# Quarters between an extra unit's two maxima, block 1's rows ahead of values, later padding, a head in halves and shifted zero products in a convolution/attention/MoE kernel on one core

## Time and profile before

| what | us |
|---|---|
| median of 3 runs | 241.24 |
| the runs | 241.24, 239.71, 246.65 |
| the profiled execution, device time | 239.72 |
| span of its trace | 237.9 |
| PE busy | 227.8 (96%) |
| DVE busy | 200.2 (84%) |
| ACT busy | 172.5 (72%) |
| POOL busy | 45.5 (19%) |

### The profile page before, as it was taken

How to read it: one execution, slowest core, us unless ns; L and a number is a source line. 1 busy time by engine, 2 the same in 40 slices (tenths; PEclk the granted TensorE clock), 3 DMA queues, 4 the chain that set the end, 5 groups by cost and what they waited for, 6 DMA issues and landing times.

```text
span 237.9 us, 6170 instructions
## 1 busy us (share of the span) xinstructions
PE 227.8 (96%) x2361; PEld 126.3 (53%) x2361; DVE 200.2 (84%) x425; ACT 172.5 (72%) x347; POOL 45.5 (19%) x80
## 2 busy tenths in 40 slices
PE   8899999999999999999999999999999998789994
PEld 6356455455555555555555555555444785558521
DVE  5899998999999999999999999999722593348874
ACT  3553759898999998899889998999996432228810
POOL 8956069400000000200000300030000000000160
PEclk9999999999999999999999999999999999999999
DMA  5005510161131120451300000000000000000002
GB/s 142 2 8 206 132 19 3 30 236 27 53 92 45 50 68 26 105 154 69 98 9 1 4 3 1 6 0 1 4 3 0 3 0 3 1 3 0 1 0 91
DMA packets 6082, 10.09 MB, mean 42 GB/s; under 512 B 2236, under 2 KB 3820, under 8 KB 5924
## 3 DMA queue, kind: packets, MB, share of 16 engines
q1 hardware_dynamic: 5908, 9.63, 13.7%
q10 hardware_dynamic: 144, 0.07, 0.1%
HBM read 6.84 MB, written 2.62 MB: 40 GB/s over the span
## 4 chain that ended last, share of the span: by engine, by line
PE 87%; POOL 5%; DVE 5%; issue 1%; ACT 1%; DVEq 0%; POOLq 0%; ACTq 0%
PE psum L598 26%; PE psum L494 17%; PE psum L530 17%; PE psum L636 4%; PE psum L916 3%; DVE half_max L1307 2%; POOL kop L958 1%; POOL qop L958 1%; PE psum L563 1%; PE psum L435 1%; PE psum L826 1%; PE psum L556 1%; PE psum L452 1%; POOL early L1039 1%; PE psum L470 1%; PE psum L816 1%
## 5 line engine op out<-in xcount | busy, mean ns | idle before, releaser
L1307 DVE TENSOR_REDUCE half_max<-psum 128x1 f32<-128x512 f32 x256 | 156.0, 678 | 2.1 <-PE psum L494 1.8
L1125 ACT ACTIVATE probs<-psum 128x512 f32<-128x512 f32 x228 | 120.0, 601 | 10.7 <-PE psum L530 6.5
L494 PE MATMUL psum<-kop,qop 64*128 64x512 f32 x256 | 87.4, 442 | 0.7 <-DVE kop L1274 0.6
L530 PE MATMUL psum<-qop,kop 64*128 64x512 f32 x256 | 83.0, 441 | 0.5 <-ACT qop L1130 0.4
L598 PE MATMUL psum<-probs,v_aug 128*32 128x256 f32 (+1 forms) x1312 | 73.1, 339 | 0.2 <-DVE o_sb L1321 0.2
L494 PEld LDWEIGHTS psum<-kop,qop 64*128 64x128 f32 x256 | 40.7, 184 | 19.9 <-DVE half_max L1307 12.6
L530 PEld LDWEIGHTS psum<-qop,kop 64*128 64x128 f32 x256 | 39.4, 184 | 20.5 <-ACT probs L1125 11.4
L598 PEld LDWEIGHTS psum<-probs,v_aug 128*32 128x32 f32 x1312 | 32.7, 109 | 30.2 <-issue 20.1
L1018 POOL CAST max_part<-negmax 128x8 fp32r<-128x8 f32 x13 | 2.5, 189 | 92.0 <-issue 81.3
L1059 POOL TENSOR_TENSOR early<-probs,early 128x512 f32<-128x512 f32 x4 | 5.1, 1275 | 56.7 <-ACT probs L1219 55.2
L1121 ACT ACTIVATE probs<-psum 128x1024 f32<-128x1024 f32 x14 | 13.4, 1027 | 0.5 <-PE psum L530 0.4
(11 more groups left out here) (192 smaller groups left out, 195.6 us busy)
## 6 DMA issues: line engine op xcount, KB each, us to landing
parts_scratch<-early SPq DMA_DIRECT2D x4, 512.0 KB, 3.8
qop<-parts_scratch SPq DMA_DIRECT2D x28, 64.0 KB
vt_sb<-in_vt SPq DMA_DIRECT2D x1, 1024.0 KB, 4.8
kop<-parts_scratch SPq DMA_DIRECT2D x14, 64.0 KB
kop<-parts_scratch SPq DMA_DIRECT2D x28, 32.0 KB
x_sb<-in_x SPq DMA_DIRECT2D x2, 256.0 KB, 3.6
q_pair<-in_q_pairs SPq DMA_DIRECT2D x1, 512.0 KB, 3.6
qop<-max_row SPq DMA_DIRECT2D x26, 4.0 KB
```

What stands on the lines that cost most here:

```text
L494: last = nc.tensor.matmul(psum[:, m % MAX_BANKS, :], qop[at, b * PP + pp, qh * NH + t * P:qh * NH + (t + 1) * P], kop[at, b * PP + pp, c * ...
L530: last = nc.tensor.matmul(psum[:, bank, :], kop[at, b * PP + pp, mt * P:(mt + 1) * P], qop[at, b * PP + pp, qh * NH:(qh + 1) * NH], start= ...
L1125: last = nc.scalar.activation(probs[:, n % P_RING, h, :], psum[:, bank, :], ACT.Exp, scale=SCALE)
L1307: V.tensor_reduce(half_max[:, i, c, h * HT + t:h * HT + t + 1], psum[:, m % MAX_BANKS, :], AX_X, ALU.max, negate=True).then_inc(S["slot_fr ...
```

## The change

- **Head in halves.** The first product takes only columns 0 to 255 of q half 0 (bank 4); columns 256 to 511 come behind k half 0, in bank 2 (`SECOND_BANK`). ACT no longer waits for DVE's `rep_dve`.
- **Quarters between the maxima.** In the extra units of g = 0 and 1 the product of queries and keys stands between the unit's two maxima; at g = 0 four products of zeros (and a wait for `v_out`) stand in front of the first.
- **Block 1's rows in front of the values** at place 8.
- **Later padding.** `pad(1)` stands in the turn of block 2, behind that block's split and three small MEMSETs.
- **Late zero products.** Two in front of the first wide stage's values, whose wait for `st_done` now stands ahead of them; five before the last output's transpose, two before `project(1)`, three for two before `mean_ready`.
- **z by twos.** Of the four transposes two stand in front of the wait for `u_ready`, two behind the layer's last product.

```diff
+CHUNK_BANKS = (4, 5, 6, 7)
+SECOND_BANK = 2
...
+        SECOND_ROWS = phase_end_from(PAIRS_OF * len(CATCH_UP))
...
+            def replicated(i, bank, first, end):
+
+                what, hf = CHUNKS[i]
+                nc.tensor.matmul(psum[:, bank, 0:end - first], w_rep[:, int(what == "k"), :],
+                                 x_sb[:, hf * NH + first:hf * NH + end], start=True, stop=True).then_inc(S["rep_full"], 1)
+
             pe.wait_ge(S["w_rep_ready"], 1)
-            for i, (what, hf) in enumerate(CHUNKS):
-                if what == "k":
-                    pe.wait_ge(S["k_rep_ready"], 2)
-                pe.wait_ge(S[f"in_x{hf}"], 16)
-                nc.tensor.matmul(psum[:, 4 + i, :], w_rep[:, int(what == "k"), :], x_sb[:, hf * NH:(hf + 1) * NH],
-                                 start=True, stop=True).then_inc(S["rep_full"], 1)
-                if i == 0:
-                    rep_constants()
+            pe.wait_ge(S["in_x0"], 16)
+            replicated(0, CHUNK_BANKS[0], 0, QB)
+            rep_constants()
+            pe.wait_ge(S["k_rep_ready"], 2)
+            replicated(1, CHUNK_BANKS[1], 0, NH)
+            replicated(0, SECOND_BANK, QB, NH)
+            pe.wait_ge(S["in_x1"], 16)
+            replicated(2, CHUNK_BANKS[2], 0, NH)
+            replicated(3, CHUNK_BANKS[3], 0, NH)
...
             def after_pair(p):
 
+                if p == SECOND_ROWS:
+                    small_work(p)
                 if p in values_goal:
                     values_until(values_goal[p])
-                small_work(p)
+                if p != SECOND_ROWS:
+                    small_work(p)
...
                     if part_ == 0:
+                        max_half(v, 0)
+                        if g == 0:
+                            pe.wait_ge(S["v_out"], 2)
+                            fill(FILL // 2, PV_BANK, 0, True)
                         pe.wait_ge(S["in_wqk1"], 16)
                         half_queries_and_keys(1, hf, 0, st_free(("qk", hf, 0)))
+                        max_half(v, 1)
                     else:
+                        max_half(v, 0)
                         half_queries_and_keys(1, hf, 1, st_banks(st_index["qk", hf, 0])[0]).then_inc(S["st_full"], 1)
-                    for c in range(HALVES):
-                        max_half(v, c)
+                        max_half(v, 1)
...
             units(first_wide + 2, first_wide + 3)
+            pe.wait_ge(S["st_done"], wide_at)
+            keep_warm(2, WIDE_SMALL)
             values_until(2 * (first_wide - 1))
-            pe.wait_ge(S["st_done"], wide_at)
             rows_of_max(LAST, WIDE_SMALL).then_inc(S["late_rows_full"], 1)
...
             values_until(2 * UNITS)
+            keep_warm(5, PROJ_BANKS[1])
             output_to_tokens(LAST_OUT, ATTN_T_BANKS[1]).then_inc(S["last_full"], 1)
             project(0)
             attn_to_channels(1)
             attn_to_channels(2)
+            keep_warm(2, PV_BANK)
             project(1)
...
-            keep_warm(2, PV_BANK)
+            keep_warm(3, PV_BANK)
             pe.wait_ge(S["mean_ready"], 1)
...
                     by_image(7, w_l, tt_l if l else eye2_sb).then_inc(S["tt_full"], 1)
+                    if l < 2:
+                        tokens_to_channels(4 * l)
                     pe.wait_ge(S["u_ready"], l + 1)
                     by_image(5, w_l, u_l).then_inc(S["gram_full"], 1)
                     if l < 2:
-                        tokens_to_channels(l)
+                        tokens_to_channels(4 * l + 2)
...
                     pool.wait_ge(S["parts1"], hf + 1)
-                    if hf == HALVES - 1:
-                        pad(1)
+                if blk == DIRECT:
+                    pad(1)
...
             act.wait_ge(S["rep_full"], 2)
-            first_part(1, 0, NH)
-            act.wait_ge(S["rep_dve"], 1)
-            first_part(0, QB, NH)
+            first_part(1, CHUNK_BANKS[1], 0, NH)
+            act.wait_ge(S["rep_full"], 3)
+            first_part(0, SECOND_BANK, QB, NH)
```

More of the change, by code:

```diff
@@ L545, in first_rows, with fill @@
                 rows_of_max(blk, st_free(("max_r", blk, 0))).then_inc(S["st_full"], 1)
-            def fill(bank, at, start):
-                for _ in range(FILL):
+            def fill(n, bank, at, start):
+                for _ in range(n):
                     nc.tensor.matmul(psum[:, bank, at:at + P], idle[:, 0:P], idle[:],
@@ L671, in _ @@
                     pe.wait_ge(S["parts0_in"], 2 * HALVES)
-                    fill(ST_BANKS[1], 0, True)
+                    fill(FILL, ST_BANKS[1], 0, True)
             first_rows(0)
@@ L794, in _, with tokens_to_channels @@
             last.then_inc(S["gram0_full"], 1)
-            def tokens_to_channels(c):
-                for t in range(4 * c, 4 * c + 4):
-                    last = nc.tensor.transpose(psum[:, PROJ_BANKS[c], (t % 4) * P:(t % 4 + 1) * P], z[:, t, :], ident)
-                last.then_inc(S["zt_full"], 1)
+            def tokens_to_channels(first):
+                for t in range(first, first + 2):
+                    last = nc.tensor.transpose(psum[:, PROJ_BANKS[t // 4], (t % 4) * P:(t % 4 + 1) * P], z[:, t, :], ident)
+                if t % 4 == 3:
+                    last.then_inc(S["zt_full"], 1)
             def by_image(bank, left, right):
@@ L1072, in _, with first_part @@
                 nc.scalar.activation(rep_rows(w_rep, 1, i), head_weights(1, i), ACT.Copy).then_inc(S["k_rep_ready"], 1)
-            def first_part(i, first, end):
+            def first_part(i, bank, first, end):
                 what, hf = CHUNKS[i]
                 w = int(what == "k")
-                nc.scalar.activation(rep_part[:, i, first:end].bitcast(F32R), psum[:, 4 + i, first:end], ACT.Identity,
+                nc.scalar.activation(rep_part[:, i, first:end].bitcast(F32R), psum[:, bank, 0:end - first], ACT.Identity,
                                      bias=rep_cols[:, 4 + w:5 + w], scale=rep_cols[:, 2 + w:3 + w]).then_inc(S["rep_act"], 1)
@@ L1082, in _ @@
             act.wait_ge(S["rep_full"], 2)
-            first_part(1, 0, NH)
-            act.wait_ge(S["rep_dve"], 1)
-            first_part(0, QB, NH)
+            first_part(1, CHUNK_BANKS[1], 0, NH)
+            act.wait_ge(S["rep_full"], 3)
+            first_part(0, SECOND_BANK, QB, NH)
             for i in (2, 3):
-                act.wait_ge(S["rep_full"], i + 1)
-                first_part(i, 0, NH)
+                act.wait_ge(S["rep_full"], i + 2)
+                first_part(i, CHUNK_BANKS[i], 0, NH)
             act.wait_ge(S["rep_cols_ready"], 3)
-            nc.scalar.activation(rep_q1, psum[:, 4 + BY_POOL_CHUNK, :], ACT.Identity,
+            nc.scalar.activation(rep_q1, psum[:, CHUNK_BANKS[BY_POOL_CHUNK], :], ACT.Identity,
                                  bias=rep_cols[:, 0:1]).then_inc(S["rep_act"], 1)
@@ L1268, in _, with second_part @@
             dve.wait_ge(S["rep_part_ready"], 1)
-            def second_part(i, first, end):
+            def second_part(i, bank, first, end):
                 what, hf = CHUNKS[i]
@@ L1274, in second_part @@
                 V.scalar_tensor_tensor(out=(kop if w else qop)[:, 0, hf * NH + first:hf * NH + end],
-                                       in0=psum[:, 4 + i, first:end], scalar=rep_cols[:, w:w + 1],
+                                       in0=psum[:, bank, 0:end - first], scalar=rep_cols[:, w:w + 1],
                                        in1=rep_part[:, i, first:end], op0=ALU.add, op1=ALU.add).then_inc(S["rep_dve"], 1)
-            second_part(0, 0, QB)
+            second_part(0, CHUNK_BANKS[0], 0, QB)
             dve.wait_ge(S["rep_act"], 1)
-            second_part(1, 0, NH)
+            second_part(1, CHUNK_BANKS[1], 0, NH)
             dve.wait_ge(S["rep_act"], 2)
-            second_part(0, QB, NH)
+            second_part(0, SECOND_BANK, QB, NH)
             dve.wait_ge(S["rep_act"], 3)
-            second_part(2, 0, NH)
+            second_part(2, CHUNK_BANKS[2], 0, NH)
             def denominators(blk):
@@ L1351, in _ @@
             late_copy(LATE + 1)
-            dve.wait_ge(S["rep_full"], len(CHUNKS))
+            dve.wait_ge(S["rep_full"], len(CHUNKS) + 1)
             dve.wait_ge(S["qk_full"], HALVES)
```

4 lines of the change are left out of this document (2 added, 2 removed).

## The result

| | before | after |
|---|---|---|
| median, 20 runs each | 240.43 | 237.86 |
| fastest run | 239.17 | 237.33 |
| profiled execution | 239.72 | 237.35 |
| span of its trace | 237.9 | 235.5 |

The ratio of after to before is 0.9918, with a 95% interval of 0.9894 to 0.9943: 0.8% faster, clear of noise and under the 2% that the forecast called about what can be told from no change. The forecast was 238.5, in a range of 237.0 to 241.8. The four rows of the table don't move alike: 2.57 us by the medians, 1.84 by the fastest runs, 2.37 by the profiled executions and 2.4 by their spans; the part on the prediction says why.

A forecast was written before the change was run, and what follows sets the result against it. The prediction took DVE to bound the maxima stage and ACT the wide stage. Head -0.2, quarters -0.3, rows -0.4, padding -0.25, zero products +0.1 and +0.05, z -0.2 sum to -1.2: 239.72 to 238.5 us, range 237.0 to 241.8.

The forecast's parts named there:

- the 2% class: Whole kernel: a change within about 2% (4.8 us), which a measurement can't tell from no change; chance 0.91.
- the account of the maxima stage: Maxima stage, 10.14 to 169.07 us: DVE bounds it at 0.60 us a reduction, with only about 3.5 us of slack.
- everything reaches its bound: Rival, whole kernel: all gains reach their bounds, 2.5 us together, so 237.2; needs no late second maximum; chance 0.06.
- Room of 1 us to block 3: Later padding: MEMSETs run from about 43 to 50, block 3's maxima are ready about 51.1, leaving 1 us.
- anything won before 43.47 would be lost: Block 2's split, held by POOL's padding until 43.47: earlier gains after block 1's split at 31.72 would be lost again.
- PE's 0.40 goes, and of DVE's 0.69 some 0.3 stay: Block 1's rows: PE's wait at 34.93 vanishes, DVE's delay at 36.71 shrinks; -0.4 us, bounds 0 and -0.69.
- what is late next: Quarters at g = 0: the second maximum comes at 26.4, DVE is ready at 26.03, so some 0.3 us late.
- as long as the fast pace sets in when it does now: Head: condition on the forecast of -0.2 us and its bounds of 0 and -0.5.
- The slow rival: Head: fast pace waits until after about 9 us, costing 3.0 us there, so 241.8 in all; chance 0.10.
- the last rival: Other executions: late zero products stop clock falls in PE's gaps; median gains over 2% at the same 238.5; chance 0.04.
- Absorbed: Rival: a shifted DVE finds PE late elsewhere; only padding and z stay, less 0.15 for zero products: 239.4; chance 0.18.

## Why the prediction was right, and where it was not

The direction, the 2% class and the range held, and so did the account of the maxima stage. The size did not: the profiled execution moved by -2.37 us against -1.2 forecast, the fastest runs by -1.84, the ratio gives 0.8% or about -2.0, and the medians of 20 runs each -2.57. The profiled 237.35 is nearer to the rival *everything reaches its bound* (237.2, a chance of 0.06) than to the forecast, and not by the way the rival names: the quarters stayed short of their bound, the rows and the head went beyond theirs. About 0.5 us of the 2.37 is luck of the one profile (the head, below).

*Right, and shown by undoing:* the maxima stage stands on DVE and everything behind is relative to it, so that each 0.1 us shows at the end (quarters 0.39 in the trace, 0.32 in fastest runs; rows 0.78 and 0.78). POOL's padding held block 2's split, and its move lets the rows pass (0.33 alone, 1.11 with the rows). Room of 1 us to block 3 (1.03). z by twos, 0.2. Zero products at the last transpose hide (forecast +0.1, measured 0); the two in the wide stage, put at 0, cost 0.06.

*What passes through the padding: one step, not three.* The prediction has the 0.9 us of head, quarters and rows pass only because of the later padding, and says that anything won before 43.47 would be lost. But POOL's chain starts at block 1's `negmax` and takes 12.5 us from there (30.94 to 43.47 before, 33.52 to 46.05 with the early padding), so it moves along with whatever is won ahead of that `negmax`. Only the rows, which lie inside it, were held. The sum of the forecast doesn't change by this.

*The rows, -0.4 forecast, -0.78 measured.* The step "PE's 0.40 goes, and of DVE's 0.69 some 0.3 stay" failed. It counted PE's wait of 0.40 and not that the score behind the wait ran alone; in the new order it runs beside a maximum, and the second 0.4 us go too. The measured -0.78 lies outside the bound of -0.69 by 0.1. This is the largest mis-sized term that the kernel owes to the change itself.

*The quarters, -0.3 against -0.39.* The mechanism held, but "what is late next" was too dark: no idle time of 0.3 appears before the second maximum. The four zero products cost 0.20 where the step had 0.3.

*The head, -0.2 against -0.81, outside the bound of -0.5.* The bound was tied to "as long as the fast pace sets in when it does now", and it did not: the rise of the granted clock is stored at 5.65 us in the profile before and at 4.19 in the one after. At 4.19 PE still works at the idle products, which are the same in both kernels, and the first product of the changed head starts only at 4.52; so the change can't have caused this earlier rise, and what it gave is luck of that execution. The nearest pair with like moments is the kernel before (rise at 5.65, first reduction at 10.14) and the halved head with the rows behind (5.52, 9.86): 0.28 us, of which the earlier rise may have a part. So the forecast's 0.2 was near for the split itself, and some 0.5 of the 0.81 come from the clock. This fits the table of the result: 2.37 less 0.5 is close to the 1.84 of the fastest runs. What the old head does behind a rise near 4.2 us no profile shows.

With the halved head the first reduction is at 9.20 to 9.86 in four profiles (rise at 4.1 to 5.5) and at 11.75 to 12.20 in four others (rise at 9.4 to 10.3); with the old head at 10.14 to 10.29 in three (5.65 to 5.87) and at 12.14 in one (10.4). The Trainium skill, "TensorE: Matmul & The Clock Gate", Part 1, has the moment vary by about 0.5 us from run to run. The traces agree that it varies, but not with the size: within the early group it spreads by 1.8 us, and the late group lies 3.5 us and more behind it, which costs about 2.5 us of total time.

*The slow rival was real, but not for the kernel as a whole.* It had 0.10 as the case that decides the median. Its price was 3.0 us from the head; the measured one is 2.7 (12.03 against 9.33), and it meets part of the executions: 6 of the kernel after's 18 runs below 243 lie at 239.7 to 240.3, 12 at 237.3 to 237.9. Whether the halved head makes it more frequent is the more important question. Of the eight kernels with the halved head and 30 idle products 30 of 77 runs lie 2 us or more above their kernel's fastest, against 2 of 16 of the two with the old head and the rest of the change (the kernel with four more products, 0 of 5, is not in this sum). The old head also stands in the kernel before and in the padding alone: 11 of 71 and 1 of 8. On each chip the halved head has more: 14 of 28 against 3 of 32, 6 of 21 against 5 of 23, 4 of 10 against 6 of 40. That points to yes, as the rival argued. It is counted by times, not by profiles, and so not proven. What the split is worth in the median is therefore not shown: 237.97 with the old head (six runs, none late), 237.86 with the new. The median of the 12 early runs is 237.5, so that it looks like 0.5 in those; but their early rises, which are not of the split's making, are in that number. By the 0.3 it gives and the 2.5 us that a late head costs, a share of late runs higher by more than about an eighth would make it a loss on average (an estimate). The prediction gave the rival 0.10 and the median a single value; a share of executions was what it needed.

*Other executions.* The medians differ by 0.7 us more than the fastest runs, although the kernel after has late heads. A likely source shows in the lists of runs. On the three chips of the experiments 18 of 71 runs of the kernel before below 243 us have a mean granted clock of 0.986 or 0.993, and 3 of 10 with the early padding; of the 87 such runs of the kernel after and of the nine others that have both rows in front and padding later, none has (one of 243.2 with 12 idle products lies just above that limit). The one of these that was profiled is that of the early padding: 3.4 us at the 1.2 GHz level, and 11.35 us from block 0's to block 1's `negmax` for 10.00. So something like the last rival did happen, but not by its cause: three of those kernels lack the late zero products. With the padding alone it is 1 of 8, with the rows behind 0 of 9; why these falls go stays open. The longer falls, in the runs above 243 us, remain in both kernels.

*Absorbed* is refuted for the main stage: nothing of quarters, rows and padding was lost up to the end. No version tried beats the kernel after beyond the intervals; leaving zero products out (0.2 us in block 1, 0.1 at the end by the traces) is the one step that looks worth trying.

## What to carry to other kernels

Before pricing a step that makes an engine earlier, look for a chain on a helper engine that runs beside it with a fixed length (here MEMSETs that stood ahead of a small urgent job), and find its start: what is won between its start and its end is lost until the chain is shortened, and what is won ahead of its start passes anyway. If a product waits alone, ask what it would have run beside; the wait and the lost company both come back. And compare kernels with a cold start by groups of runs, not by one profile each.

## What was not expected of the hardware

The pace of the first products falls into two groups, in runs of one and the same kernel (237.3 to 237.9 and 239.7 to 240.3 us). Over all kernels the granted clock rises at 4.1 to 5.9 us in seven profiles and at 9.4 to 10.4 in seven others (one of these with 12 idle products), about 2.5 us of total time apart. The printed row of the granted clock reads 1.00 in both; the stored moment of the rise and the length of the passes (0.47 or 0.87 us for 512 columns) tell. The clock can also fall while PE is busy: with four more products in the head it fell at 27.0 us though PE was busy for at least 0.97 us of each of the four microseconds before. A delay can leave no idle time in DVE's records: 16 reductions in 9.88 for 9.68 us was all that the four zero products left to see.
